# GpSimd begins the row gathers of a unit only when the nine gathers of the unit before have landed

## What is computed

```python
# image x projected: xproj (32+2 padded rows and columns, 16 groups of 32 channels)
# per pixel, group and tap (3x3): position px, py from an offset, weight m from a softmax
v00, v01, v10, v11 = four neighbours of (py, px) in xproj, 32 channels each
samp = (v00 * (1 - wx) + v01 * wx) * (1 - wy) + (v10 * (1 - wx) + v11 * wx) * wy
out[pixel, group] = sum over the 9 taps of samp * m
```

## Time and profile before

| | us |
|---|---|
| median of three runs | 17378.5 |
| lowest, highest | 17342.42, 17394.83 |
| span of the profiled execution (first to last instruction; the page gives no total for it) | 17321.9 |
| GpSimd busy in it | 9147.2 (53%) |
| VectorE busy | 9764.5 (56%) |
| TensorE matmuls busy | 8991.0 (52%) |
| ScalarE busy | 4946.3 (29%) |

### The profile page before, as it was taken

How to read it: one execution, slowest core, us unless ns; L and a number is a source line. 1 busy time by engine, 2 the same in 40 slices (tenths; PEclk the granted TensorE clock), 3 DMA queues, 4 the chain that set the end, 5 groups by cost and what they waited for, 6 DMA issues and landing times. The chain is left out here.

```text
span 17321.9 us, 109853 instructions
## 1 busy us (share of the span) xinstructions
PE 8991.0 (52%) x32544; PEld 4339.4 (25%) x32544; DVE 9764.5 (56%) x9864; ACT 4946.3 (29%) x13537; POOL 9147.2 (53%) x9221
## 2 busy tenths in 40 slices
PE   6754554445634564445634555445634556344447
PEld 3322222222312232222312222122312223111113
DVE  7646745476546854477445855467554765433333
ACT  2314421243214421143203422144212432111111
POOL 0025655656546664656555664556555665555551
PEclk7976777667766777767866777667866777677778
DMA  1021112211132112211132112211122111322111
GB/s 58 8 59 42 44 47 66 93 42 51 38 88 66 45 49 62 89 43 52 36 75 79 43 49 59 93 41 46 45 74 78 44 50 51 89 81 71 61 60 45
DMA packets 905633, 1002.04 MB, mean 58 GB/s; under 512 B 697681, under 2 KB 707921, under 8 KB 893074
## 3 DMA queue, kind: packets, MB, share of 16 engines
q0 software_dynamic: 294912, 604.57, 12.3%
q1 hardware_dynamic: 610066, 389.88, 7.4%
HBM read 814.38 MB, written 179.39 MB: 57 GB/s over the span
## 5 line engine op out<-in xcount | busy, mean ns | idle before, releaser
L131 POOL DMA_INDIRECT gat<-corner_tables,idx x9216 | 9146.7, 992 | 7868.6 <-DVE dcn L168 3093.5
L795 PE MATMUL PS<-hc,ident 128*128 128x512 f32 (+2 forms) x4096 | 2018.1, 653 | 483.0 <-DVE hc L839 309.8
L168 DVE TENSOR_REDUCE dcn<-gat 128x32 f32<-128x1152 f32 x1024 | 2162.7, 2112 | 127.2 <-ACT gat L148 83.5
L148 ACT ACTIVATE gat<-gat,wts 128x32 f32<-128x32 f32 x8752 | 1979.4, 308 | 525.6 <-issue 523.8
L862 DVE TENSOR_TENSOR_SCAN hs<-dA,PS 128x1024 f32<-128x1024 f32 x672 | 1531.5, 2279 | 37.5 <-issue 4.4
L162 DVE TENSOR_TENSOR gat<-gat,wts 128x1152 f32<-128x1152 f32 (+3 forms) x1024 | 1093.8, 1068 | 567.1 <-DMA gat<-corner_tables,idx 397.3
L795 PEld LDWEIGHTS PS<-hc,ident 128*128 128x128 f32 x4096 | 1036.8, 286 | 1125.1 <-issue 640.8
L1071 PE MATMUL PS<-ident,E 128*128 128x128 f32 x4096 | 676.5, 313 | 909.1 <-ACT ET L1140 484.0
L1216 DVE COPY ET<-PS 128x512 f32<-128x512 f32 x512 | 348.7, 681 | 1204.6 <-remote 693.6
L839 DVE TENSOR_TENSOR hc<-hs,PS 128x1024 f32<-128x1024 f32 x672 | 803.0, 1195 | 169.7 <-remote 85.6
L1740 PE MATMUL PS<-late_M,wp 128*32 128x512 f32 x4480 | 640.2, 723 | 458.3 <-DVE wp L1804 202.5
(11 more groups left out here) (251 smaller groups left out, 11848.4 us busy)
## 6 DMA issues: line engine op xcount, KB each, us to landing
gat<-corner_tables,idx POOLq DMA_INDIRECT x9216
corner_tables<-xp SPq DMA_DIRECT2D x1024, 64.0 KB, 2.2
D<-in_dist_dram SPq DMA_DIRECT2D x8, 4096.0 KB, 12.7
keep_scratch<-X SPq DMA_DIRECT2D x15, 2048.0 KB, 11.6
weighted<-M SPq DMA_DIRECT2D x56, 512.0 KB
late_M<-weighted SPq DMA_DIRECT2D x7, 4096.0 KB
wqkv<-in_qkv_w_dram SPq DMA_DIRECT2D x8, 3072.0 KB, 10.2
X<-keep_scratch SPq DMA_DIRECT2D x12, 2048.0 KB, 14.9
```

Of the source, the lines that this page charges most:

```text
L131: nc.gpsimd.indirect_dma_start(bd.gat[n % self.NG][:, k * 4 * CG:(k + 1) * 4 * CG], None, bd.rows, bass.IndirectOffsetOnAxis(ap=bd.idx[:, ...
L148: ins = nc.scalar.activation(block, block, ACT.Copy, scale=weights[:, i:i + 1])
L168: nc.vector.tensor_reduce(bd.dcn[m % 2][:, g * CG:(g + 1) * CG], gat[:].rearrange("p (k c) -> p c k", c=CG), AX.X, ALU.add).then_inc(self. ...
L795: mm = nc.tensor.matmul(PS[:, p.ybank(d, h), 0:p.hl], self.ident[:], src[:, j, h * p.hl:(h + 1) * p.hl], start=(c == 0 and j == 0), stop=( ...
```

## The change

Before the first gather of a unit (except unit 0 of an image) POOL waits until the buffer of the preceding unit has received its nine gathers. The order of the instructions, the buffers and the other waits stay. One semaphore per buffer counts 16 for each gather of 128 rows, so nine gathers of the k-th use of a buffer are there at 16 x 9 x k.

```diff
         for i, (n, k) in enumerate(rows):
             m, g = n // G, n % G
+            if k == 0 and n:
+                pool.wait_ge(self.gathered[(n - 1) % self.NG], 16 * KP * ((n - 1) // self.NG + 1))
             if k == 0 and n >= self.NG:
                 pool.wait_ge(self.summed, n - self.NG + 1)
```

## The result

| | before | after |
|---|---|---|
| median of the runs (4 each, same chip) | 17381.85 us (17342.42 to 17394.83) | 16042.25 us (15988.80 to 16069.55) |
| span of the profiled execution | 17321.9 us | 16042.2 us |
| granted TensorE clock, mean | 0.726 | 0.743 |

The ratio is 0.9236, with a 95% interval from 0.9214 to 0.9257: the kernel is 7.6% faster. The forecast was 17396 us, with a range of 17345 to 17475.

What follows compares the result with a forecast made beforehand. No engine was full; gathers were taken as background work nearly always ahead. Costs of 5.3 + 9.2 + 3 = 17.5 us on the 17321.9 span, plus 56.6 carried over to the median, gave 17396 us, range 17345 to 17475.

Steps and rivals of the forecast that it cites:

- The covers: Output projection, next image's convolutions, start of attention: DVE waits longer for something else, so late gathers there cost 0.
- Price of a wait: POOL at each unit boundary: 1.32 us per unit, from DVE's 1.62 to see a landing less POOL's 0.30 step.
- Slack: One image, 6985 to 8974: 183 us of added waits fit into 477 us of POOL idle for DVE and ACT.
- DVE's waits for gathers: Whole span: to grow from 403.0 to about 560 us, most of it hidden in projection, convolution and attention.
- Place A: Group norm of the second image, pipeline starting empty: unit 2 seen 3.9 to 6.7 us later, middle 5.3 us.
- B: End of the first background image: POOL is the bound, nothing hides 7 waits of 1.32, 9.2 us.
- C: Beginning of the scan's preparation: 14 units without enough pauses, 1.8 us late in the tightest image; 3 us over all seven.
- Stalls fall otherwise: Rival: unexplained "remote" stalls may move, seven stages by 8 us either way, 17340 or 17455 us; chance 0.12.
- The loads get faster: Rival: held gathers leave DMA engines to the loads, 10 to 29 us back, 17376 us at 20; chance 0.12.
- What would show it wrong: Waits on gathers inside scans or mid-attention, POOL landing pauses well over 1.6 us, or gather-free stages changing by tens of us.

Runs made afterwards that it cites:

- the seventh run: Against the kernel before: only one gather of nine per unit, the other eight left out (sampled values wrong); 13227.12 us, ratio 0.7641.
- the quarter rows: Against the kernel before: gather rows of 128 bytes instead of 512, taken from another tensor (values wrong); 17160.83 us, ratio 0.9916.

## Why the prediction was wrong, point by point

- **The failed step is in the first part:** "So the gathers are background work that is nearly always ahead. A wait added on POOL costs time only where that lead is used up." The first half is right. The second counts only who waits for a gather's data. The gathers also slow PE, ACT and SP while they go at full pace, with nobody waiting for them, and a later gather can therefore be worth time. In the sum this was a term put at nothing. The wait never gets its value from a landing; it brings the mean pace from 1.25 to 1.43 us per gather. By the seventh run eight gathers of nine cost 4.1 ms; I had counted the 403.0 us of DVE's waits.
- **The covers were not fixed.** "DVE has then still 19.09 us to wait for its first add" and the 39.48 in the other image, "43.94 us" and "47.67 us": I took these as time of the foreground under which a late unit may hide. In the seventh run, where few gathers run beside them, DVE idles at the same places of the seven background images 9.2 to 9.7 us in the projection, 29.8 to 33.9 before the first row of the steps and 25.3 to 29.7 before the first copy of the keys. What stood above that was there only with the gathers. After the change all three covers are used up (timeline of DVE, at the places of the 43.94, the 47.67 and the 39.48):

```profile
1303.00 0.21 DVE L718 TENSOR_TENSOR xd<-PS,bc 32x64 f32<-32x64 f32 x1 [1.45 <-issue]
...
2225.84 0.68 DVE L1201 TENSOR_TENSOR kk<-PS,cols 128x512 f32<-128x512 f32 x1
...
6635.06 5.35 DVE L1527 SCALAR_TENSOR_TENSOR X<-PS,cols,X 128x512 f32<-128x512 f32 x8
```

  The second and third follow a unit with no idle at all. That this cost so little is because the foreground became faster at the same time: the projection's stage is 57 us shorter. It does so elsewhere too. The view of all waits, before the change (engine, tile, line, what ended the wait, us in total, times, longest), for ACT at L1162 in attention and for DVE at L830 in the scans:

```profile
ACT rrow L1162 <- remote: 734.1, 80, 17.6
...
DVE PS L830 <- remote: 608.0, 82, 26.3
```

  and after, where the lines are L1164 and L832:

```profile
ACT rrow L1164 <- remote: 323.0, 55, 18.0
...
DVE PS L832 <- remote: 226.6, 66, 14.5
```

- **Price of a wait (1.32 us):** too low, but not where it mattered. The boundary shows 1.90 where 0.30 stood, so 1.6 us per unit; 2157.1 us over 967 waits is 2.2 each with the long landings. Even 2.2 us for 1016 units, 2.2 ms, went for less than nothing. Waits that named the landings were forecast for some 700 units and came in 967.
- **Slack:** forecast was that POOL's idle for DVE shrinks from 3093.5 to 2200. It shrank to 432.7: the foreground got 177 us shorter in that image (1145 us over the seven middle ones, 164 each), and the slack of 477 us went with it. The balance was drawn with a foreground held constant.
- **DVE's waits for gathers:** forecast 560, measured 1576.1, and ACT's 676.3 were not forecast at all. Both are now real costs, as the +8.6 us before the projection shows; they are what the gain of 177 us in that image is net of.
- **Place A** (+5.3 us) came as forecast. Counted from POOL's first gather, DVE begins the third unit at 1198.38 - 1155.64 = 42.7 us before and at 1213.11 - 1163.94 = 49.2 after, 6.4 us later, within the 3.9 to 6.7 of the sum; the normalised image behind it is 6.4 us later too.

```profile
1213.11 1.36 DVE L164 TENSOR_TENSOR gat<-gat,wts 128x1152 f32<-128x1152 f32 x1 [4.67 <-DMA gat<-corner_tables,idx]
```

  The first convolution right behind it (L607, L609 after) then takes 49.1 us from its first row to its last instead of 98.1, which is far more than what A costs. The terms of the sum were thus not what failed, as far as A shows. B and C were forecast at 9.2 and 3 and can't be told from the gain around them.
- **The rivals:** none was this. "Stalls fall otherwise" pointed at the right rows (a wait called "remote", 19.09 in one image and 39.48 in another with the same program) and priced them as chance, 60 us either way, where the question would have been what makes them. "The loads get faster" had the sign and 10 to 29 us; the quarter rows bound anything of bytes at 0.8%. In all I gave "faster" 0.06.
- **What would show it wrong:** I named waits on gathers inside scans and attention, and stages without gathers that change. The first came. The second did not: the tail is 263.5 and 263.7, and the stretch ahead of the first gather 1155.6 and 1163.9.

**What stays open.** What it is that fills up is not shown. The steps are of 0.70 us per instruction, on several engines at once, ended by nothing that the profile records, and tied to the number of gathers (or their 32 packets each) per microsecond. It is not the gathers' own transfers that pile up: counted off in the packed trace, the last of a gather's sixteen packets of 4 bytes ends 2.26 us after the gather's start in the median for the first gather of a run, 2.28 for the 50th to 70th and 2.26 for later ones. A late supply of instructions is not seen either: the trace has packets of a queue of that kind (271 of 16 KB), and they take 1.02 us in the median before and 1.11 after; a single one lies between 7000 and 7110, where ACT and PE step for some 80 us. And every time here, those of the experiments too, is that of an execution whose span and clock were recorded, with the packets of the gathers among what the profile records; whether the recording has a part in the steps, no run shows. Nor do the counted steps make up the gain. They are 235, 483 and 132 us on engines that overlap, against 1280 us of span. The rest is in shorter waits such as the 381 us of L830 and the 411 of L1162 above, which may have the same cause without showing five equal steps in a row; for that there is only the order of the table.

## What to carry to other kernels

Before calling a stream of DMAs background work, look at the idle time of the engines that don't wait for it, above all rows that end in "issue" or "remote" and come in equal steps, and run the kernel once with most of the stream left out: the difference is its real price. If that is large, slow the stream evenly, as far as its consumers allow, before making anything faster; the best pace is just short of where they start to set the end. And a stall that is used as a cover in a sum has to be explained first; the same run with the stream left out shows how much of it is really there.

## What the runs showed of the hardware that was not expected

- Gathers issued by GpSimd at one per 1.25 us made other engines step at multiples of 0.70 us per instruction, from 3 to 90 us into such a stretch until at most 11 us after it. At 1.34 us there was less of it (ACT 161 us instead of 483), at 1.44 us none. The gathers' own landings did not become later in such a stretch (2.26 us from the start in the median, first or 70th).
- A quarter of the bytes (0.8% of the time) and half of the rows (1.4% slower, with the gathers 3% closer together) did not help: the cost goes with the number of gathers. Each moved as 32 packets in all three sizes.
- A gather of 64 rows takes POOL 903 ns, one of 128 rows 944 ns, so almost nothing of it is per row.
- POOL goes on 1.90 us after its last gather ends when it waits for that gather's landing, where DVE took 1.62.
